# Graph network on one core: a sixth of the weight products of the setup moved from VectorE to GpSimd

## The reference

```python
h = jnp.maximum(_layernorm(x, axis=-1), 0.0)
x = x + _L0_gnn_ref(h, edge_index, ...)        # sum of h[src] over dst, two dense layers, norm
h = jnp.maximum(_layernorm(x, axis=-1), 0.0)
x = x + _L1_gnn_ref(h, src, dst, ...)          # attention over the edges, 8 heads
h = jnp.maximum(_layernorm(x, axis=-1), 0.0)
x = x + _L2_gnn_ref(h, edge_weight, ...)       # sums weighted by exp(edge_weight - max), both ways
h = jnp.maximum(_layernorm(x, axis=-1), 0.0)
x = x + _L3_gnn_ref(h, edge_index, ...)        # mean of h[src] over dst, two dense layers
```

## Time and profile before

| what | value |
|---|---|
| median of 3 runs | 1258.97 us (1258.36 to 1259.93) |
| the profiled execution | 1256.01 us, of which the span of the core is 1254.1 us |
| TensorE, busy share of the span | 88% |
| VectorE, busy share of the span | 52% |
| GpSimd, busy share of the span | 11% |
| mean granted clock of TensorE | 0.954 |

### The profile page before, as it was taken

The page is one execution under the profiler, slowest core; times in us unless marked ns, Lnnn a source line. Parts: engine busy times, 40 slices in busy tenths (PEclk is TensorE's granted clock), DMA queues, the critical chain, the costliest instruction groups (busy, mean ns, idle before and its releaser), DMA issues.

```text
span 1254.1 us, 17427 instructions
## 1 busy us (share of the span) xinstructions
PE 1102.4 (88%) x5880; PEld 698.9 (56%) x5880; DVE 646.8 (52%) x1835; ACT 419.7 (33%) x711; POOL 144.0 (11%) x112
## 2 busy tenths in 40 slices
PE   1378877779999999989999999999996998899998
PEld 0134444445555445547777777776453798555543
DVE  6877787784017840026666666665619525700033
ACT  2501233330006341016555555555234523610000
POOL 0000000002654440000000000001315403000000
PEclk9998777779999999999999999999999998999999
DMA  5001467778886111100000000005301005000001
GB/s 153 0 0 42 129 173 208 201 213 269 274 281 210 56 34 34 34 0 1 2 1 2 1 1 2 2 1 178 119 1 34 9 13 194 34 1 1 9 33 40
DMA packets 67233, 93.65 MB, mean 75 GB/s; under 512 B 5145, under 2 KB 56032, under 8 KB 67158
## 3 DMA queue, kind: packets, MB, share of 16 engines
q1 hardware_dynamic: 67158, 92.65, 23.4%
HBM read 58.03 MB, written 34.60 MB: 74 GB/s over the span
## 4 chain that ended last, share of the span: by engine, by line
PE 72%; DVE 12%; DMA 6%; issue 5%; ACT 3%; SPq 2%; DVEq 0%; ACTq 0%
PE PS L459 8%; PE PS L669 7%; PE PS L493 7%; PE PS L652 7%; PE PS L817 7%; PE PS L626 7%; PE PS L852 5%; DMA edge_parts<-X 5%; PE PS L597 5%; PE PS L531 5%; PE PS L504 3%; PE PS L587 3%; DVE R L1117 2%; PE PS L779 2%; PE PS L799 2%
## 5 line engine op out<-in xcount | busy, mean ns | idle before, releaser
L459 PE MATMUL PS<-HT,R 125*128 125x313 bf16 (+1 forms) x636 | 178.5, 419 | 61.2 <-DVE HT L1000 27.5
L459 PEld LDWEIGHTS PS<-HT,R 125*128 x636 | 103.5, 171 | 137.0 <-issue 103.9
L1106 DVE CUSTOM_DVE_ANT_0 HT<-PS,CD 128x1250 f32<-128x1250 f32 (+1 forms) x80 | 116.3, 1454 | 55.2 <-issue 55.2
L652 PE MATMUL PS<-K,HT 128*128 128x128 f32 (+2 forms) x800 | 112.5, 280 | 15.0 <-DVE R L1117 14.4
L1008 DVE TENSOR_SCALAR HT<-BC,HT 125x314 f16 x316 | 102.0, 364 | 35.9 <-PE PS L459 30.9
L1382 ACT ACTIVATE HT<-HT,soft 128x1250 f32<-128x1250 f32 (+1 forms) x80 | 107.1, 1338 | 19.7 <-DVE soft L1109 12.6
L1285 ACT COPY X<-PS 128x626 f32<-128x626 f32 x80 | 53.6, 689 | 167.9 <-PE PS L459 102.9
L652 PEld LDWEIGHTS PS<-K,HT 128*128 128x128 f32 (+2 forms) x800 | 84.0, 140 | 43.1 <-DVE R L1117 23.6
L1362 ACT COPY R<-PS 128x512 f32<-128x512 f32 (+1 forms) x120 | 64.8, 574 | 121.5 <-PE PS L652 119.5
L626 PE MATMUL PS<-R 64*128 64x512 f32 (+3 forms) x480 | 95.8, 531 | 4.8 <-DVE soft L1106 3.1
L669 PE MATMUL PS<-R 128*64 128x128 f32 (+2 forms) x1600 | 94.3, 273 | 0.0
(11 more groups left out here) (211 smaller groups left out, 1357.1 us busy)
## 6 DMA issues: line engine op xcount, KB each, us to landing
edge_parts<-X SPq DMA_DIRECT2D x160, 156.5 KB, 3.5
X<-edge_parts SPq DMA_DIRECT2D x15, 626.0 KB, 5.6
R<-edge_parts SPq DMA_DIRECT2D x15, 626.0 KB, 5.7
CD<-edge_sums SPq DMA_DIRECT2D x1, 6250.0 KB, 20.9
CD<-edge_parts SPq DMA_DIRECT2D x10, 469.5 KB, 4.5
CD<-edge_parts SPq DMA_DIRECT2D x3, 1565.0 KB, 11.6
X<-in_x SPq DMA_DIRECT2D x2, 2304.0 KB
edge_sums<-X SPq DMA_DIRECT2D x5, 625.0 KB, 6.2
```

Of the source, the lines that this page charges most:

```text
L459: return mm(bank(b0 + h, QUART), stat, hot, start=first, stop=True, skip_group_check=True)
L652: m = nc.tensor.transpose(PS[0:rows(j), o:o + n], Pb[u % 2][a][0:n, j * P:j * P + rows(j)], ident[0:n, 0:n])
L1106: ve.tensor_tensor_reduce(Pb[s][a][0:n], PS[0:n, a * N:(a + 1) * N], cd[0:n, t, :], 1.0, -3e38, ALU.add, ALU.max, soft[0:n, s, a:a + 1]).t ...
```

## The change

The third multiplication of VectorE covers 16 of the 32 rows of block 3 instead of all 32. The other 16 rows (rows 112 to 127 of `dst_oh`) are made by GpSimd in one multiplication of 16 x 320 = 5120 elements per partition, which waits for `wpart[2]` by a new semaphore. TensorE waits for it (`last_part`) ahead of the window loop. To stay within the number of semaphores, the two additions per tile of GpSimd now count on one semaphore (`tile_summed`, two per tile) instead of two, and ScalarE no longer waits for `tiny`, a constant that VectorE writes right after the window loop.

```diff
             for t in range(T):
-                sp.wait_ge(sem("tile_summed"), t + 1)
+                sp.wait_ge(sem("tile_summed"), 2 * t + 2)
...
             pe.wait_ge(sem("win_table"), 1)
+            pe.wait_ge(sem("last_part"), 1)
...
-            link(ve.tensor_copy(wpart[2], rem2))
+            ve.tensor_copy(wpart[2], rem2).then_inc(sem("wpart"), 1)
+            dve.wait_ge(sem("wpart"), 1)
...
-            shape = [EC, 4 * SUB, NC]
             for q in range(3):
-                i = ve.tensor_tensor(dst_oh[0:EC, (q + 1) * 4 * SUB:(q + 2) * 4 * SUB, :],
-                                     dst_oh[0:EC, 0:4 * SUB, :],
-                                     wpart[q].unsqueeze(1).to_broadcast(shape), ALU.mult)
+                m = 4 * SUB if q < 2 else 2 * SUB
+                i = ve.tensor_tensor(dst_oh[0:EC, (q + 1) * 4 * SUB:(q + 1) * 4 * SUB + m, :],
+                                     dst_oh[0:EC, 0:m, :],
+                                     wpart[q].unsqueeze(1).to_broadcast([EC, m, NC]), ALU.mult)
...
-            ve.memset(gate[:, 0:1], 1e-18).then_inc(sem("tiny"), 1)
+            ve.memset(gate[:, 0:1], 1e-18)
...
-            act.wait_ge(sem("tiny"), 1)
...
+            pool.wait_ge(sem("wpart"), 1)
+            gp.tensor_tensor(dst_oh[0:EC, 14 * SUB:16 * SUB, :], dst_oh[0:EC, 2 * SUB:4 * SUB, :],
+                             wpart[2].unsqueeze(1).to_broadcast([EC, 2 * SUB, NC]), ALU.mult).then_inc(sem("last_part"), 1)
+
             for t in range(T):
                 s = stage[t % 2]
                 pool.wait_ge(sem("parts_in%d" % (t % 2)), 48 * (t // 2 + 1))
-                gp.tensor_tensor(s[0], s[0], s[1], ALU.add).then_inc(sem("sum_own"), 1)
-                pool.wait_ge(sem("sum_own"), t + 1)
+                gp.tensor_tensor(s[0], s[0], s[1], ALU.add).then_inc(sem("tile_summed"), 1)
+                pool.wait_ge(sem("tile_summed"), 2 * t + 1)
                 gp.tensor_tensor(s[0], s[0], s[2], ALU.add).then_inc(sem("tile_summed"), 1)
```

## The result

| kernel | median | runs | lowest to highest |
|---|---|---|---|
| before | 1258.97 us | 9 | 1254.06 to 1260.80 us |
| changed | 1263.65 us | 9 | 1260.59 to 1264.79 us |

The ratio is 1.0036, with a 95% interval of 1.0021 to 1.0052: the change costs 4.5 us, between 2.6 and 6.5 us. The profiled execution of the changed kernel took 1263.85 us, its span 1261.9 us.

The account below looks back on a forecast made before the run. TensorE was taken to bound the whole kernel, VectorE the setup that changes. An 8.6 us delay less 2.66 us spared gives +5.9 us, 1258.97 + 5.9 = 1264.9 us; range 1260.5 to 1268.5 us.

Parts of the forecast that it names:

- The bound: Setup: VectorE is the only link on the chain, and its shifts move the window loop and the end one to one.
- What VectorE is spared: Third multiplication in the setup: halving it takes 2.81 us instead of 5.47, sparing 2.66 us.
- GpSimd's time: GpSimd's multiplication of 5120 elements in the setup: taken as 10.4 us, with bounds of 6.1 and 12.7 us.
- The start: GpSimd's multiplication begins 0.17 us after the cast writing `wpart[2]`, at 34.71 us, 1.7 us before VectorE's first multiplication.
- Turns: Setup: VectorE's first multiplication waits for GpSimd's whole instruction and ends at 50.4 us, 8.6 us later.
- L936 and ScalarE's cover: Setup: PSUM-reading L936 keeps its length beside GpSimd; ScalarE's table load ends at 59.1 us, still covered by 0.9 us.
- The sum: Setup and whole kernel: 8.6 us later less 2.66 us spared, +5.9 us, giving 1264.9 us on the median.
- the ports don't collide: Rival, setup: GpSimd works hidden beside VectorE's multiplications, so 2.66 us are gained, 1256.3 us; chance 9%.
- GpSimd comes late: Rival, setup: GpSimd starts after VectorE's first multiplication and delays the second; +6.7 us, 1265.7 us; chance 7%.
- GpSimd is far slower: Rival, setup: bf16 multiplication on GpSimd takes 21 us, twice the f32 rate; +16.6 us, 1275.5 us; chance 5%.
- the delay is absorbed within 2 us of before: Rival, behind the setup: something such as the window stores hides the delay, within 2 us of before; chance 4%.

Follow-up runs that it names:

- e1: Changed kernel, but GpSimd's 16 rows are not computed, only set to zero at the program's start; median 1256.23 us against 1257.96 before, ratio 0.9985.
- e2: Changed kernel, but VectorE makes all 32 rows and GpSimd's multiplication goes into an unread spare tile; median 1265.71 us, ratio 1.0064 to before.
- e4: Changed kernel, but VectorE makes all rows and GpSimd only fills a spare tile with zeros; single run 1257.12 us, before median 1257.96.
- e3: Changed kernel, but GpSimd starts only just after VectorE's first multiplication has begun; single run 1264.28 us, before median 1257.96.
- e7: Changed kernel with GpSimd's share cut to two rows, plus six comparison rows of block 0 on GpSimd; single run 1256.08 us, before 1255.16.
- e8: Kernel before, with the load of the first window bounds moved right behind VectorE's second multiplication; single run 1258.53 us, before 1255.16.

## Why the prediction was right, point by point

**The bound.** Right. The setup is VectorE's, and each microsecond there moved the loop: e1 gained 2.66 us of setup and 1.7 us in the median, e2 lost 7.96 and 8.1 us. No part of the delay was absorbed within what the intervals can tell.

**What VectorE is spared.** 2.66 us predicted, 2.66 us measured.

**GpSimd's time.** This term was mis-sized. I took 10.4 us, between 9.7 us by L1484 and 11.0 us by the f32 rows; it took 9.84 us, that is (9.84 - 0.19) / 5120 = 1.88 ns an element. The row with a bf16 input was the right neighbour, and the second bf16 tensor and the 16 short rows together added 0.1 us at most. That is 0.56 us too much in the sum.

**The start.** Predicted 0.17 us behind the cast, measured 34.55 - 34.47 = 0.08 us.

**Turns.** Right: the first multiplication ends 5.34 us behind GpSimd, where 5.33 was predicted from the earlier trace rows; its row shows 13.41 us in the range of 13 to 15. Which trait of it decides was left open by the prediction ("L942 is both"). e4 speaks for its two inputs in SBUF: beside a GpSimd instruction that only writes it is not held, where the one-input L949 is.

**L936 and ScalarE's cover.** Right, though the prediction gave no row for the first half, that an instruction that reads PSUM is not held. The trace of before had one: L1070, with one PSUM and one SBUF input, keeps 0.69 us although GpSimd's L1462 runs from 419.89 to 421.16 us.

```profile
420.46 0.69 DVE L1070 TENSOR_TENSOR R<-PS,BC 128x512 f32<-128x512 f32 x1 [0.74 <-PE PS L531]
```

In the changed kernel L938 keeps 1.82 us. ScalarE's table load ends at 58.32 us, and the wait for L966 that follows is 1.22 us: covered still.

**The sum.** +5.9 us predicted, +5.27 us in the setup; with 9.84 us in place of 10.4 and 0.08 in place of 0.17 it would have been 5.3. The runs measured 4.5 us (2.6 to 6.5), and 1263.65 us where 1264.9 was predicted. The profiled spans differ by 7.8 us, which is more. Of the 2.5 us beyond the setup, 1.9 lie in the window loop, which takes 226.6 us from its first product to the first of L493 in the profile of before, and 228.5 us in that of after; over the eleven kernels profiled here it takes 225.7 to 230.2 us without an order by the setup, so I take it as the run's own variation. Its cause is open. The granted clock goes with it in part: of the 17 runs of before beside e1, the four shortest (1253.08 to 1254.91 us) have a mean granted clock of 0.958 to 0.963, the four longest (1259.29 to 1260.94 us) one of 0.952 to 0.955.

**The rivals.** That the ports don't collide is refuted by the 13.41 us above and by e2. That GpSimd comes late did not happen: its multiplication begins 0.08 us behind the cast. A row that belongs to the same line stands right at the start of the program (columns: count, duration in ns, first and last start in us):

```profile
L1453 POOLq MODIFY_POOL_CONFIG  x2: 11/11/11, 0.7 to 0.8; - x2
```

The load of some 6 us of which the Trainium skill speaks ("GPSIMD Engine Reference", "2.1 Instruction dispatch") would be over long before 34.5 us if it follows this row; no row shows the load itself, so where it falls, and whether there is one, stays open. That GpSimd is far slower is refuted by its 9.84 us; its price was a little low besides, since twice the 11.0 us of the f32 rows is 22 and not 21 us. That the delay is absorbed within 2 us of before is refuted by the change itself, 2.6 us or more by its interval. The price of the late rival was also a little wrong: I let the second multiplication wait, while e3 shows that L949 ahead of it waits already (7.0 us instead of 6.7).

## What to carry to other kernels

Before work is moved from VectorE to GpSimd, look at what VectorE does during that time: beside instructions that read PSUM, or beside the reduction of e7, GpSimd's time cost nothing here. Beside a long instruction with two SBUF inputs it is paid in full, and some instructions with one SBUF input wait too (L949, and L1040 in the old trace). Here 11% busy on GpSimd and the 20 us until TensorE needs block 3 looked like room, and the room was 1.8 us. Two neighbouring rows of the old trace told it, L1040 recorded with 3.47 us instead of 0.81 and L1041 with 3.99 us instead of 1.46 next to GpSimd. Their end times gave the end of the held multiplication, 5.33 us behind GpSimd's, to 0.01 us; the price was off by 0.6 us, nearly all of it through GpSimd's own duration.

## What the runs showed of the hardware

- A VectorE multiplication with two bf16 inputs in SBUF, 5.47 us, is not touched by a GpSimd fill of 10.10 us, but waits out a GpSimd multiplication of 9.84 us whole. A VectorE instruction on ten f32 elements with one input waits for either: 2.92 us and 9.83 us recorded instead of 0.16 us.
- GpSimd's speed in bf16 multiplication is 1.88 ns per element (2.11 ns with f32 inputs), and it takes 1.06 us for a comparison of 320 elements that takes VectorE 0.16 us.
- The load of 20 values (loop bounds) into VectorE's registers, 1.33 us on the chain of the kernel before, cost nothing in e8, where it is placed behind a long multiplication that is still running: the setup was 1.47 us shorter.
- VectorE instructions that read PSUM keep their time beside GpSimd: 1.82 us for six comparisons (L938), 0.55 us for those of e7 with one PSUM and one SBUF input.
